# Four value visits a quad instead of six, layer norms on ScalarE, and new tables of the order of steps

## The reference, cut to what matters

```
x = x + 0.5 * ffn(layernorm(x))
x = x + attention(layernorm(x))
x = x + 0.5 * ffn(layernorm(x))

layernorm(x) = (x - mean) / sqrt(var + 1e-5)          # over the 256 features
ffn(x)  = x @ W.T + b + sum_e gate_e * (x @ A_e.T) @ B_e.T   # top 2 of 8 experts, rank 16
attention: kv = rmsnorm(x @ W_kv) * g (rank 64), q_c = x @ W_q (rank 128)
  16 heads, content part 16 wide, rotary part 32 wide, values 16 wide
  scores = q @ k.T / sqrt(48), causal softmax over 1024 keys, out = probs @ v, out @ W_o
```

## Time and profile before

| | |
|---|---|
| median of 3 runs | 2131.92 us (2131.22 to 2135.18) |
| profiled execution: its own time | 2139.53 us |
| its span (first to last instruction) | 2137.8 us |
| instructions | 38517 |
| mean granted TensorE clock | 0.985 of full |
| PE busy | 2013.1 us |
| DVE busy | 1675.6 us |
| ACT busy | 1263.9 us |
| POOL busy | 972.0 us |

### The profile page before, as it was taken

One profiled execution on the slowest core, in us unless ns is written; L12 is line 12 of the kernel. 1 busy time (PEld: TensorE's weight loads), 2 busy tenths in 40 slices (PEclk: granted clock), 3 DMA queues, 4 the chain that ended last, 5 costly groups with the idle time before them and its releaser, 6 DMA issues.

```text
span 2137.8 us, 38517 instructions
## 1 busy us (share of the span) xinstructions
PE 2013.1 (94%) x13248; PEld 1559.8 (73%) x13248; DVE 1675.6 (78%) x4924; ACT 1263.9 (59%) x2857; POOL 972.0 (45%) x1574
## 2 busy tenths in 40 slices
PE   4799999999999999999999999999999999999995
PEld 3677777777777777777777777777777777777754
DVE  4698888777888788888888878887788877888842
ACT  4456676655665566666566555665666655665750
POOL 5543544544545544344544435452444544444511
PEclk9999999999999999999999999999999999999997
DMA  2131221223112222213212232123221222212111
GB/s 75 45 75 31 80 54 46 61 70 95 44 43 73 73 80 56 59 45 90 81 41 70 68 79 57 41 70 80 85 56 46 58 86 82 65 51 56 36 31 42
DMA packets 71666, 132.34 MB, mean 62 GB/s; under 512 B 9840, under 2 KB 28528, under 8 KB 71472
## 3 DMA queue, kind: packets, MB, share of 16 engines
q1 hardware_dynamic: 71472, 129.87, 22.7%
HBM read 40.97 MB, written 38.54 MB: 37 GB/s over the span
## 4 chain that ended last, share of the span: by engine, by line
PE 71%; DVE 17%; DMA 4%; issue 3%; ACT 2%; POOL 1%; SPq 1%; POOLq 0%; DVEq 0%; ACTq 0%
PE mx_b L673 11%; PE st_b L643 11%; PE st_b L645 10%; PE o_b L661 9%; PE wj_b L605 5%; DVE st L864 4%; PE tp_b L712 3%; DVE mx_b L820 3%; PE wp_b L697 3%; PE wj_b L576 3%; PE wj_b L607 2%; PE wp_b L694 2%; DVE xn L906 2%; DMA aoc<-ao_scratch 2%; PE wj_b L594 2%
## 5 line engine op out<-in xcount | busy, mean ns | idle before, releaser
L733 ACT ACTIVATE probs<-st_b 128x512 f32<-128x512 f32 (+3 forms) x1536 | 699.2, 490 | 516.9 <-PE st_b L645 500.7
L820 DVE CUSTOM_DVE_ANT_0 mx_b<-mx_b,tri 128x256 f32<-128x256 f32 (+3 forms) x1024 | 513.7, 511 | 79.8 <-PE mx_b L673 72.5
L643 PE MATMUL st_b<-st 113*128 113x512 f32 (+2 forms) x1536 | 566.1, 373 | 8.6 <-DMA st<-shift_scratch 6.4
L673 PE MATMUL mx_b<-st 112*128 112x256 f32 (+2 forms) x1536 | 540.3, 387 | 16.9 <-DVE mx_s L820 14.6
L645 PE MATMUL st_b<-st,k_st 112*128 112x512 f32 (+2 forms) x1536 | 530.4, 350 | 0.0
L1012 POOL TENSOR_TENSOR rot_c<-qk,cos_s 128x256 f32<-128x256 f32 x256 | 191.6, 748 | 590.2 <-ACT v_s L743 589.5
L823 DVE TENSOR_REDUCE mx_s<-mx_b 128x1 f32<-128x512 f32 (+1 forms) x512 | 334.4, 653 | 91.0 <-PE mx_b L673 87.0
L864 DVE TENSOR_TENSOR st<-tp_b,st 48x512 fp32r<-48x512 f32 x512 | 352.4, 688 | 44.3 <-ACT st L755 30.9
L673 PEld LDWEIGHTS mx_b<-st 112*128 112x128 f32 x1536 | 275.7, 190 | 131.6 <-issue 58.4
L755 ACT ACTIVATE st<-tp_b 48x512 fp32r<-48x512 f32 x512 | 302.8, 591 | 74.6 <-PE tp_b L712 63.5
L643 PEld LDWEIGHTS st_b<-st 113*128 113x128 f32 x1536 | 292.9, 191 | 55.6 <-ACT probs L733 14.1
(11 more groups left out here) (151 smaller groups left out, 2553.4 us busy)
## 6 DMA issues: line engine op xcount, KB each, us to landing
k_st<-st SPq DMA_DIRECT2D x128, 384.0 KB, 6.1
nx_scratch<-stg SPq DMA_DIRECT2D x14, 768.0 KB, 3.5
cur<-nx_scratch SPq DMA_DIRECT2D x14, 768.0 KB, 4.4
ao_scratch<-o_f SPq DMA_DIRECT2D x256, 32.0 KB, 1.7
xa<-in_x SPq DMA_DIRECT2D x15, 512.0 KB, 4.6
x_scratch<-xa SPq DMA_DIRECT2D x15, 512.0 KB, 2.8
xa<-x_scratch SPq DMA_DIRECT2D x15, 512.0 KB, 3.3
aoc<-ao_scratch SPq DMA_DIRECT2D x15, 512.0 KB, 4.3
```

Of the source, the lines that this page charges most:

```text
L643: nc.tensor.matmul(dst, k1_st[u][0:SHIFT + 1, a, P * j:P * j + P], q_st[u][0:SHIFT + 1, a, q0:q0 + w], start=True, stop=False)
L673: nc.tensor.matmul(mx_b[:, m % 2, 0:w], q_st[u][0:SHIFT, a, P * i:P * i + P], k1_st[u][0:SHIFT, a, k0:k0 + w], start=True, stop=True).then ...
L733: nc.scalar.activation(probs[:, a, PLACE[s]:PLACE[s] + n], st_b[:, a % 2, HALF - n:HALF], ACT.Exp, scale=SCALE).then_inc(exp_done, 1)
L820: nc.vector.tensor_tensor_reduce(src, src, tri[:, HALF - n:HALF], 1.0, NEG, ALU.add, ALU.max, dst).then_inc(mx_done, 1)
```

## The change

It has three parts. The value visits become `(0,1,2,3)`, `(4,5)`, `(6,7)`, `(8,9,10,11)`: four a quad, of 1280, 1024, 1024 and 1280 columns a head. The `norm` steps move from DVE to ACT as `Identity(rs * x + nb)` with `nb = -mean * rs`; POOL computes `nb` with two further instructions of 128x4 a layer norm, and raises `rstd` after the last of them. The order tables of all five engines are new. In the diff, the `norm` step shown is the new one in ACT's block; the same step is taken out of DVE's. Counts of all letters stay the same but for V of PE (192 to 128), and J and j of DVE and ACT (96 norm steps move from the one to the other).

```diff
-PV = [(s, s + 1) for s in range(0, NS, 2)]
+PV = [(0, 1, 2, 3), (4, 5), (6, 7), (8, 9, 10, 11)]
 ORDER = {
     "PE": (
-        "JJjJjJjjJJjJjjJJJJjjjJjPJPJjPJTJPTPXXTXXXXPXTXJXXPXXTJXXTPXJXXTPXXPXXFTXXXPXXSSTXXSSXXSSXPXSXSTSXSXVXXSS"
+        "JJjJJjjjJJjJjjJJJJjjjJjPjPJJjPTJPTJPXXTXXXXPXXTXXXXPXXTXXPXFXXTXJXXPXXTSXSXJXXTSSPXXSTSXSXPXXSSPXSXTSSXJX"
...
     "ACT": (
-        "BBBBBBBJBJjJjJjJjjJjJJJJjjjJjCJCJjJHHCJJHHCHHCHHCJHHCHHCHHCHHCEEHHEECEEEEHEEHCEEEEHEHECJHHCJJHHCJHHCEEHH"
+        "BBBBBJJBJjjJBJjBJjJjjjJjJJJJJjjJjjjJJjJCJCJjHHCJHHCJJHHCHHCHHCHHCJHHEECHHEECEHEHECEEEHEEHCEEHHCEEHHCHHCJ"
...
-FFN_DVE = [("stats", 0, 0), ("stats", 0, 1), ("aggr", 0), ("norm", 0, 0), ("norm", 0, 1)]
+FFN_DVE = [("stats", 0, 0), ("stats", 0, 1), ("aggr", 0)]
...
-LAT_DVE = [("stats", 1, 0), ("stats", 1, 1), ("aggr", 1), ("norm", 1, 0), ("norm", 1, 1), ("ss",), ("kvn",)]
+LAT_DVE = [("stats", 1, 0), ("stats", 1, 1), ("aggr", 1), ("ss",), ("kvn",)]
-FFN_ACT = [("evac", "tr0"), ("evac", "tr1"), ("evac", "low0"), ("evac", "low1"), ("ex",), ("evac", "gated_tr")]
-LAT_ACT = [("evac", name) for name in LAT_MM]
+FFN_ACT = [("norm", 0, 0), ("norm", 0, 1), ("evac", "tr0"), ("evac", "tr1"), ("evac", "low0"), ("evac", "low1"), ("ex",), ("evac", "gated_tr")]
+LAT_ACT = [("norm", 1, 0), ("norm", 1, 1)] + [("evac", name) for name in LAT_MM]
...
+                self.nm, self.nb = take("nm" + tag, [P, GT]), take("nb" + tag, [P, GT])
...
+                elif name == "norm":
+                    own = lanes[LANE[g]]
+                    k, part = arg
+                    if part == 0:
+                        act.wait_ge(own.rstd[k], count(g, k) + 1)
+                    for tk in range(2 * part, 2 * part + 2):
+                        last = nc.scalar.activation(own.xn[:, tk, :], own.xa[:, tk, :], ACT.Identity,
+                                                    bias=own.nb[:, tk:tk + 1], scale=own.rs[:, tk:tk + 1])
+                    if part:
+                        last.then_inc(own.normed[k], 1)
...
                     nc.gpsimd.tensor_scalar(own.ve[:, :], own.mv[:, :, 1], LN_EPS, None, ALU.add).then_inc(own.rv[k], 1)
-                    pool.wait_ge(own.rv[k], n + 1)
-                    nc.gpsimd.tensor_tensor(own.rs[:, :], own.ve[:, :], powers[:, :], ALU.pow).then_inc(own.rstd[k], 1)
+                    nc.gpsimd.tensor_scalar(own.nm[:, :], own.mv[:, :, 0], -1.0, None, ALU.mult)
+                    pool.wait_ge(own.rv[k], 2 * n + 1)
+                    nc.gpsimd.tensor_tensor(own.rs[:, :], own.ve[:, :], powers[:, :], ALU.pow).then_inc(own.rv[k], 1)
+                    pool.wait_ge(own.rv[k], 2 * n + 2)
+                    nc.gpsimd.tensor_tensor(own.nb[:, :], own.nm[:, :], own.rs[:, :], ALU.mult).then_inc(own.rstd[k], 1)
```

More of the change, by code:

```diff
@@ new lines @@
+        "XXSSTXSXSVXXSSJXXSSTJXXSSPXSXSPXXSSPXXSSTXSXSVXXSJSXSTJXSSXPJXSFXSJXXSSTXSXPXVSSXXTSSXXPSXSXPSXSXTSJXSXV"
+        "JFXSXSJXXSSTXSXSXPXSXSTXSXSXVXXSSTXSXSPXXSSPXSXSXSSXJSSXXP",
+        "SSXJSSXJSXSJXSXSTXSSVXFXPSSXXTSSXXSSXXPSSXXTSSVJXXSSJXXSSJXXSSTPSSVFXXSSXTXSXSXPJXXSSJVXJXXSSXJXXSSTXSXS"
+        "PSSXTXSJSXSPXSXSTSXSXSXPXSXSTSXSXVXXSSPXSTJXSSXPJXSXSXJXSSFXJSXXTPXXSSXVSSXXTSSXPJSXSJXSXSJFXXSSTXSVXXSS"
+        "TXSXPJXXSSPJXXSSJXXSSJXXSSTXSVXJXSSTXSXSPXXSSPXSSXPSXSXVSXSXTSXSXSJXSSXTSPJFXSXSPSSTSXXXSSXXPXJXSXSJXSXS"
@@ new lines @@
+        "JXSXJSXSTSVPFXXSSTVJXXSSJXXSSJXXSSTXSXSPXXSSTXSXSVXXSSJXXSSTJXXSSPXSXSPXXSSPXXSSTXSXSVXXSJSXSTJXSSXPJXSF"
+        "XSJXXSSTXSXPXVSSXXTSSXXPSXSXPSXSXTSJXSXVJFXSXSJXXSSTXSXSXPXSXSTXSXSXVXXSSTXSXSPXXSSPXSXSXSSXJSSXXP",
+        "SSXJSSXJSXSJXSXSTXSSVXFXPSSXXTSSXXSSXXPSSXXTSSVJXXSSJXXSSJXXSSTPSSVFXXSSXTXSXSXPJXXSSJVXJXXSSXJXXSSTXSXS"
+        "PSSXTXSJSXSPXSXSTSXSXSXPXSXSTSXSXVXXSSPXSTJXSSXPJXSXSXJXSSFXJSXXTPXXSSXVSSXXTSSXPJSXSJXSXSJFXXSSTXSVXXSS"
+        "TXSXPJXXSSPJXXSSJXXSSJXXSSTXSVXJXSSTXSXSPXXSSPXSSXPSXSXVSXSXTSXSXSJXSSXTSPJFXSXSPSSTSXXXSSXXPXJXSXSJXSXS"
@@ L147 @@
+        "FXXSTXSXSXSXSXSTXSXSVXXSSXXSSXXSSXSXSXSSXSXSXSSXSXVSXSXSXSSXSXSSXSSSSFSSVSSSSSSSSSSVSJSSJSSSSSVSSJSSJSSJ"
+        "SSJSSSSSSVJJJjjjjjjjjj",
     ),
     "ACT": (
[L149 to L151 removed]
@@ new lines @@
+        "EEJEEJEEJEEHHCEJEEEHEEHCEEEEHHEECJEEEEEEHHCEEEEHJJEEJHEEJCJEEJEEHHEECEEHEJEEHCEEEHEHECEEHEEHEJJEECJEEHHJ"
+        "EECJEEJEHHCJEEEEHHEECJEEEEEEHEHEJJEECJEEHHJCEEJEEJEEHEHJEEEECEECEHEHEEEEHEHEECEEHEHCEEEEHEHCJJEEJEEJEEJE"
+        "JEHHJCEEEEHHCJEEEEEEHHEECEEHHEEEEEEEECEEHHCEEEEHEHECJJEJEEHJEEHCJEEJEEHEHCJEEHHEECEEEEHHJEECEEEEHEHECEEH"
+        "EHEEEEECEEJEEJEECJEEHH",
+        "EEJEEJEEJEEHHCEJEEEHEEHCEEEEHHEECJEEEEEEHHCEEEEHJJEEJHEEJCJEEJEEHHEECEEHEJEEHCEEEHEHECEEHEEHEJJEECJEEHHJ"
+        "EECJEEJEHHCJEEEEHHEECJEEEEEEHEHEJJEECJEEHHJCEEJEEJEEHEHJEEEECEECEHEHEEEEHEHEECEEHEHCEEEEHEHCJJEEJEEJEEJE"
@@ new lines @@
+        "MLLMMJMMLLoMMoMoLMMfLoMnMMMJJMMJJMJLJLJoJoMMJLMMJLMMoMoMLfMMLJnMMJMMMMLMLMMMLMMLJMMJMMJMMMMMMMM",
+        "LLMMMMMJMLLJfJJonMMJoJMMJoMMLLMJMJoJMMLLooMMooJMMJMMJfLLJJnMMMMLMMMMLMMMMMMJMLLMJMMLMLMMMMLMLMMJJMJMLLMM"
+        "oMooMMfoMLMMLMnMMJMJJJMJMJMJLJLJoJMMLMLooMoJMMfJnMJJMJMLLMMMMMMLMMLMMMJMMLJLMMMMMMMMLLMMooMMoMLLMoJMMfLL"
+        "JnJJMJMMLMMLMMMMMMMMMJMJJJfJLJLJoJoJnJMMoLLoMMJMMJMMMMLLMMMMLLMMJMMJMMJMMJMMLLMMJMMLLoMMoMoLMMfLoMnMMMJJ"
+        "MMJJMJLJLJoJoMMJLMMJLMMoMoMLfMMLJnMMJMMMMLMLMMMLMMLJMMJMMJMMMMMMMM",
@@ L201 @@
+        "ssakaJssJJkasskaJsskJJJcasskcsasJJJkasskassJJk",
+        "ssakaJssJJkasskaJsskJJJcasskcsasJJJkasskassJJJkasskaJsJsJkasskassJJkasskasskassaJjajJj",
     ),
@@ L900, in _ @@
                                             ALU.mult).then_inc(folded, 1)
-                elif name == "norm":
-                    k, part = arg
-                    if part == 0:
-                        dve.wait_ge(own.rstd[k], count(g, k) + 1)
-                    for tk in range(2 * part, 2 * part + 2):
-                        last = nc.vector.tensor_scalar(own.xn[:, tk, :], own.xa[:, tk, :], own.mv[:, tk, 0:1], own.rs[:, tk:tk + 1],
-                                                       ALU.subtract, ALU.mult)
-                    if part:
-                        last.then_inc(own.normed[k], 1)
                 elif name == "route":
```

114 lines of the change are left out of this document (45 added, 69 removed).

## The result

The changed kernel takes 2099.55 us (median of 4 runs, 2096.72 to 2101.24), the one before 2131.57 in the runs beside it (4 runs, 2127.12 to 2135.18). The ratio is 0.9849, 95% interval 0.9828 to 0.9871: 32 us faster. The forecast was 2110 us with a range of 2090 to 2133, so the time lies in the range, 10 us under the forecast. The profiled execution took 2099.12 us, 40.4 less than that of before; 8.0 of these are what the profiled execution of before had over the median of 2131.57.

A forecast was written before the change was run, and what follows sets the result against it. PE, 94% busy, was taken as the bound, DVE second. Profiled: 2139.5 - 21.8 - 5 + 3 + 1.5 + 0.7 = 2117.9; from the median, 2131.9 - 21.6 = 2110 us, range for 8 in 10 2090 to 2133, forecast's own 2099 to 2121.

The forecast's parts named there:

- Visits, -21.8: On PE, two visits fewer in each of 32 quads save 0.34 us each: -21.8 us, bounds -8 to -25.
- The long visit, 0: On PE, first and last visits of a quad take 2.27 us; waits this adds taken as 0, bound 0 to +10.
- DVE's relief, -5: Norms leave DVE, so PE waits less for it before mx: -5 us, bounds 0 and -46.
- rival 1: DVE's relief is worth more, most of 46 us of waits go and tables use the slack: about 2090; chance 0.15.
- ACT's norms, +3: Norms in ACT's strict order delay exponentials and so PE's next scores: +3 us, bounds 0 and +10.
- Head, +1.5: At the kernel's start, a longer norm chain and more ACT time before evacuations: +1.5 us reaches the end, 0 to +5.
- Tail, +0.7: At the end, the last job's transpose waits longer for its layer norm, through POOL and ACT: +0.7 us.
- The tables, "some us either way": New order tables of the engines change waits alone; not priced, room of some us either way.
- "issue" idle before value matmuls: Sign on PE: weight-load idle with no semaphore behind it, before value matmuls, near 78 us instead of 116.8.
- Rival 2: Visits are saved, but a 2.27 us visit starves DVE and PE then waits for it: about 2126; chance 0.17.
- Rival 3: ACT stands at the norm waiting for POOL, holding up PE: 2135 to 2160; sign, that wait over 20 us; chance 0.12.
- Rival 4: On ACT, Identity needs another table set, two loads for each of 48 layer norms, 123 us: 2233; chance 0.01.

The follow-up runs named there:

- old_merge4: The kernel before with four value visits a quad in its old tables, nothing else changed: 2193.4 us, ratio 1.0271 to the kernel before.
- split6_adjacent: The changed kernel with its first and last visits each cut in two, the halves directly behind each other: 2094.9 us, ratio 0.9834 to the kernel before.
- split6: The changed kernel with its first and last visits each cut in two, one other PE step between the halves: 2139.0 us, ratio 1.0029 to the kernel before.
- three: The changed kernel with three visits a quad and DVE's work on the value banks three steps later: 2254.6 us, ratio 1.0544 to the kernel before.
- old_act: The kernel before with norms on ACT and POOL's two extra instructions, six visits, old order otherwise: 2183.3 us, ratio 1.0221 to the kernel before.
- split8: The changed kernel with all four visits cut in two, one other PE step between the halves: 2161.8 us, ratio 1.0133 to the kernel before.
- old_merge4_late: old_merge4 with DVE's work on finished value banks three steps later in all quads but the last: 2234.1 us, ratio 1.0470 to the kernel before.

## Why the prediction was right, and where its steps were not

The time fell, and it lies in the range, but the number is in part luck. In the profiled executions, in which the terms were added up, 21.6 us were forecast and 40.4 measured. Between the medians it is 32, because the profiled execution of before took 8 us more than its median, and 2099.55 stands at the very edge of the forecast's own range, 2099 to 2121. The main term, the visits, came out. What was missing is waits of PE that no term held.

- **Visits, -21.8: size right, as a cost of PE.** old_merge4 gives -21.6 in the fixed parts, split6_adjacent, with four groups and no fall of the clock, too (50.5), the kernel after -17.2. The cause, the change between value matmuls and other work, is shown by split6 against split6_adjacent. The upper bound of 25 was too low for what a cut costs in time when the tables stay as they are: 0.47 to 0.65 us each.
- **The long visit, 0: right** at 2.28 us, but not for the very last one, which took 3.8 us at a lower clock, 1.5 more than the others. The timeline of after:
```profile
2044.44 3.88 PE L660 MATMUL o_b<-probs,v_s 128*17 128x512 f32 x32 [1.07 <-POOL probs L1000]
2048.25 0.66 PE L598 MATMUL wj_b<-ident,xn 128*128 128x128 f32 x4
```

- **DVE's relief, -5: this term was mis-sized.** I took little of 46 us because PE's weight loads idled little for DVE, and left out PE's own 15.5 us for `mx`. Weight loads give back 16.6 us and PE 10.1, part of it the same time. With the norms on DVE, the new tables lose 42 us, an upper end. So part of rival 1's mechanism is at work, DVE's relief with tables that use it; the time lies between its 2090 and the forecast. How much of the fall in these waits is the relief and how much the tables no run separates.
- **ACT's norms, +3.** The duration was 592 ns and not the 385 of the row; by the Trainium skill's rule that the prediction quotes ("ScalarE: Activation LUTs", section "What ACT_TABLE_LOAD costs") it was 585, and the trace agrees. ACT's busy time is 1347.1, inside 1338 to 1379 all the same: 83 us more, where 192 x 592 ns are 114, because neighbours on ACT overlap in the trace (four norms in a row take 2.07 us, not 2.37). PE's wait for `xn` in the body grew from 7.8 to 13.1: +5, inside the bounds of 0 to 10.
- **POOL:** 225 and 202 ns against 228. Right.
- **Head, +1.5: too much.** The first transpose starts 0.93 us later (24.53 us, before 23.60), but this does not reach the body. The timelines of before and of after:
```profile
57.10 1.98 PE L613 MATMUL wj_b<-cur,wkvq_s 128*128 128x512 f32 x4 [0.69 <-ACT cur L795]
59.77 2.00 PE L619 MATMUL wj_b<-wkvq_s,cur 128*128 128x64 f32 x16 [0.69 <-ACT cur L795]
...
57.13 3.34 PE L612 MATMUL wj_b<-cur,wkvq_s 128*128 128x512 f32 x4 [0.69 <-ACT cur L804]
```
The matmuls that follow the last one begin at 61.16 us in the kernel after: 1.4 later than 59.77, which looks like the forecast and isn't. These four matmuls ran at a lower clock (3.34 us, not 1.98). Before, the clock fell 7 us later, and at the next job's same matmuls the kernel after is ahead (68.53 against 68.71). Part of the early delay was made good because PE ran the matmuls from 41 to 44 us at a low clock before and at full clock after.
- **Tail, +0.7:** the last transpose idled 6.75 us where it was 5.59, +1.2; from the first transpose of lane 0's last job to the end it is 0.8 longer. Right.
- **The tables, "some us either way": the missing term.** They removed 18.4 us of PE's waiting for the attention output. Every kernel in the old tables keeps 13 to 18 us of it, those in the new ones none or 0.3 (three: 4.4). It stood in the trace of before, and I had not read it: I had looked at PE's weight loads alone and not at PE's own waits. The clock's 8.4 us had no term either. The split between tables and parts can't be made by adding: a part alone in the old tables costs 2 to 3%, and taking one out of the new ones costs about 2%.
- **Rival 2** (a long visit starves DVE, PE waits for DVE): not here, PE's waits at `mx` fell; it is what happens in old_merge4, to 46.5 us. **Rival 3:** ACT waited 25.7 us for POOL, over the mark of 20, 11.2 of them in the head, and the kernel is faster: the mark was too low, since PE waited only 13.1 us for `xn` in the body. Slower was right in the old tables (old_act), but there by what stands behind the norms on ACT. **Rival 4:** one table load. Wrong, as expected.
- **A sign that was wrong:** "issue" idle before value matmuls was to fall to 78 us. It rose to 129.6, and is 113.9 in split6, 128.0 in split6_adjacent, 142.2 in old_merge4. With the most visits, in split8, it is lowest, 89.5. It also counts weight loads inside a visit (of the three that idle in the visit at 833.78 us of before, 0.37, 0.31 and 0.31 us, two are inside), so it never measured the number of visits. Busy time of the value matmuls fell by 11.5 us, in the band of 10 to 15.

Open: why four visits in the old tables make PE wait 46.5 us for DVE at `mx`, now that DVE's wait at the value banks is ruled out; how much of the 32 us tables made for one part alone would keep; and how much of the shorter waits is DVE's relief.

## What to carry to other kernels

In a kernel whose engines follow a written order, a local change is priced by its own cost on the bounding engine plus every semaphore wait of that engine, longest first, DMA waits included, because new tables can take them away; and it can't be tested in tables made for something else, where each part here cost 2 to 3%. To learn whether a cost belongs to a change of work or to the number of steps, put the same steps next to each other and then one step apart. Gather the value matmuls into fewer visits as long as the engines and buffers behind them don't make PE wait for more than what each visit saves, 0.3 us or more here.

## What the runs showed of the hardware that I had not expected

A pause of PE can cost more than its length. After some waits of 1.4 to 4.7 us inside the body, the granted clock was at 1.2 GHz for a few us while PE was full, and the eight matmuls behind the wait of 3.64 us took 3.18 us instead of 1.54. The windows of before around the longest wait, which ended at 1489.88 us:
```profile
1488.00:1492.00 4.00, 2.12 (x5) 1.79 (x6) 0.00 (x0) 0.00 (x0) 0.00 (x0) 0.50 0.34 59
1492.00:1496.00 4.00, 4.00 (x14) 3.20 (x14) 1.85 (x4) 1.20 (x2) 0.00 (x0) 0.68 0.00 0
```
The length of a wait alone doesn't tell: before has a fall at 109 us behind waits of 0.8, 0.6 and 0.4 us, split6_adjacent has a wait of 1.7 us and no fall in its body, and a wait of 2.2 us in before had none behind it. Over the runs this loss went with the waits: 0 to 12 us in the five kernels with 42 to 58 us of waits, 14 to 50 us in those with 66 to 139. It grew by 29 us from old_merge4 to old_merge4_late, which differ by a small move and by 41 us. That the waits are the cause of the loss is read from the timelines; no run changed the one without the other.
